# A two-layer graph-attention kernel: all scores of a quad and all attentions of the preceding quad in one bundle over eight PSUM banks, rows finished two steps behind

## The reference, cut to what matters

```python
def layer(x, adj, Wq, bq, Wk, bk, Wv, bv):          # layer 1; layer 0 also has Wo, bo
    q = (x @ Wq + bq).reshape(b, n, H, HD)          # H = 8, HD = 64; k and v alike
    scores = jnp.einsum('bihd,bjhd->bhij', q, k) / jnp.sqrt(jnp.float32(HD))
    scores = scores + mask[None, None, :, :]        # -1e9 where adj == 0
    weights = jax.nn.softmax(scores, axis=-1)
    return jnp.einsum('bhij,bjhd->bihd', weights, v).reshape(x.shape)
x = _layernorm(x + layer0(x) @ Wo + bo)
x = _layernorm(x + layer1(x))
```

## Time and profile before

| | |
|---|---|
| median of three runs | 3045.7 us |
| the profiled execution | 3046.8 us |
| its span, first to last instruction | 3045.0 us |
| TensorE busy | 3000.5 us (99%) |
| VectorE busy | 1915.4 us (63%) |
| ScalarE busy | 1560.9 us (51%) |
| GpSimd busy | 1366.4 us (45%) |
| mean granted TensorE clock | 0.994 of full speed |

### The profile page before, as it was taken

One profiled execution on the slowest core, in us unless ns is written; L12 is line 12 of the kernel. 1 busy time (PEld: TensorE's weight loads), 2 busy tenths in 40 slices (PEclk: granted clock), 3 DMA queues, 4 the chain that ended last, 5 costly groups with the idle time before them and its releaser, 6 DMA issues.

```text
span 3045.0 us, 58516 instructions
## 1 busy us (share of the span) xinstructions
PE 3000.5 (99%) x18956; PEld 2464.5 (81%) x18956; DVE 1915.4 (63%) x7060; ACT 1560.9 (51%) x5135; POOL 1366.4 (45%) x1285
## 2 busy tenths in 40 slices
PE   8999999999999999999999999999999999999996
PEld 6888888888888888888888888888888888888885
DVE  4656656565656566565656666666667666667665
ACT  4353535454444535353545556555556555565553
POOL 3454545545454545445454534343433333434332
PEclk9999999999999999999999999999999999999997
DMA  4443444444444445344445555555555555555554
GB/s 147 117 133 106 135 114 125 116 120 120 124 125 124 126 112 136 107 130 120 119 119 148 145 160 147 147 155 161 147 162 149 148 154 158 150 162 151 148 156 125
DMA packets 410914, 414.58 MB, mean 136 GB/s; under 512 B 46064, under 2 KB 308464, under 8 KB 410608
## 3 DMA queue, kind: packets, MB, share of 16 engines
q1 hardware_dynamic: 409312, 410.17, 48.8%
q10 hardware_dynamic: 1296, 0.67, 0.1%
HBM read 142.22 MB, written 100.66 MB: 80 GB/s over the span
## 4 chain that ended last, share of the span: by engine, by line
PE 98%; issue 1%; DVE 0%; DMA 0%; ACT 0%; SPq 0%; POOL 0%; POOLq 0%; DVEq 0%
PE ring L307 47%; PE ring L315 35%; PE ps_score L342 8%; PE ring L353 8%; DMA prob<-w_k 0%; DVE prob L628 0%; ACT k_all L487 0%; PE ps_score L315 0%; DMA prob_t<-turned 0%; DVE turned L646 0%; POOL rstd L829 0%; SPq L207 0%; DVE stats L681 0%; DVE x_res L676 0%; DVE w_lo_k L591 0%
## 5 line engine op out<-in xcount | busy, mean ns | idle before, releaser
L506 ACT ACTIVATE prob<-prob,neg_max 128x128 f32<-128x128 f32 x2048 | 791.7, 389 | 182.7 <-DVE neg_max L628 182.7
L822 POOL TENSOR_TENSOR prob<-prob,inv_sum 128x512 f32<-128x512 f32 x512 | 527.7, 1052 | 546.3 <-DVE inv_sum L636 546.3
L494 ACT ACTIVATE q_all<-ring,bq_col 128x512 f32<-128x512 f32 x256 | 176.6, 690 | 900.2 <-PE ring L307 900.2
L829 POOL TENSOR_TENSOR rstd<-var_eps,minus_half 128x1 f32<-128x1 f32 x256 | 169.5, 662 | 859.2 <-DVE var_eps L685 858.5
L628 DVE CUSTOM_DVE_ANT_0 prob<-ps_score,mask 128x128 f32<-128x128 f32 x2048 | 442.5, 285 | 153.6 <-PE ps_score L342 153.4
L646 DVE STREAM_TRANSPOSE turned<-prob 128x512 f32<-128x512 f32 x512 | 343.0, 696 | 305.7 <-DMA prob_t<-turned 214.5
L812 POOL TENSOR_TENSOR xt_lo<-x_raw,xt_hi 128x512 fp32r<-128x512 f32 x254 | 339.3, 1343 | 243.9 <-DVE xt_hi L603 243.9
L307 PE MATMUL ring<-xt_hi,w_hi_k 128*128 128x512 f32 x1024 | 399.0, 390 | 14.9 <-DVE w_lo_k L591 14.9
L307 PE MATMUL ring<-xt_hi,w_hi_q 128*128 128x512 f32 x1024 | 413.0, 403 | 0.0
L315 PE MATMUL ring<-w_hi_v,xt_hi 128*128 128x512 f32 x1024 | 412.7, 403 | 0.0
L307 PE MATMUL ring<-xt_lo,w_hi_q 128*128 128x512 f32 x1024 | 399.9, 391 | 0.0
(11 more groups left out here) (66 smaller groups left out, 4707.3 us busy)
## 6 DMA issues: line engine op xcount, KB each, us to landing
prob_t<-turned SPq DMA_DIRECT2D x1024, 128.0 KB, 2.7
x_res<-x_tok SPq DMA_DIRECT2D x256, 256.0 KB, 3.0
x_raw<-x_feat SPq DMA_DIRECT2D x254, 256.0 KB, 3.1
x_feat<-x_turned SPq DMA_DIRECT2D x512, 64.0 KB, 2.1
x_tok<-x_bias SPq DMA_DIRECT2D x128, 256.0 KB, 2.3
prob_t<-x_bias SPq DMA_DIRECT2D x512, 64.0 KB, 2.2
out<-x SPq DMA_DIRECT2D x128, 256.0 KB, 2.6
prob<-w_k SPq DMA_DIRECT2D x2, 512.0 KB, 7.7
```

What stands on the lines that cost most here:

```text
L494: act.activation(q_all[:, m, :], ring[bank][:], ACT.Identity, bias=bq_col[layer][:, m:m + 1]).then_inc(q_set, 1)
L506: last = act.activation(prob[b][:, i, n, :], prob[b][:, i, n, :], ACT.Exp, bias=neg_max[b][:, i, n:n + 1], scale=-1.0, accum_out=row_sum[b ...
L822: pool.tensor_tensor(prob[b][:, i], prob[b][:, i], inv_sum[b][:, i, :].unsqueeze(2).to_broadcast([P, NC, NODES]), ALU.mult).then_inc(norm_ ...
```

## The change

The eight PSUM banks become one ring. The scores of a quad take all eight (`score_bank(b, e)` is bank 2b + e). In a step TensorE runs keys (banks 7, 4, 5, 6), queries (banks 0 to 3), the values of graph 0 (bank 7), the scores of all four graphs, right behind them the attentions of all four graphs of quad a = s - 1 (banks 0 to 3, each as soon as the scores that lay there are masked), the values of graphs 1 to 3 (banks 4 to 6), and in layer 0 the four out projections. The four small bundles of a step become one of 128 instructions.

The rows of a quad are finished a step later, f = s - 2, so there is a step more (66). That takes more buffers: the high and low attention parts are there for each graph (`at_hi`, `at_lo`), the values of graph 0 twice (`v_first`), and the carried attention of layer 1 goes into `at_lo[b]` instead of `prob_t[b]`. `w_new` is given up for room; the second-layer weights are copied to internal DRAM tensors in step 0, and in step 31 loaded into the low-part buffers and split there, all six halves at the end of the step.

The order on the other engines is changed with it. DVE in step s: turn_blocks of graphs 2 and 3 of quad a between the finishes of quad f, then all four `x_high` of quad s + 1, then all masks of quad s, then the attentions of quad a. SP in step s: two raw loads, turn_probs(a, 2), the stores of graphs 0 and 1 of quad f, turn_probs(a, 3), the stores of graphs 2 and 3, the other two raw loads, turn_probs(s, 0), carries 0 and 1, turn_probs(s, 1), carries 2 and 3. POOL and ACT follow the same order. Waits that changed are shown below.

```diff
 # TensorE
+                    for m in range(NC):
+                        if m == 0:
+                            need(pe, masked_set, 2 * QB * s)
+                        else:
+                            need(pe, v_set, QB * a + m + 1)
+                        keys(s, m)
...
+                        if layer_of(s - 2) == 0:
+                            pe.wait_ge(sum_set, QB * (s - 2) + m + 1)
+                        elif layer_of(s - 2) == 1:
+                            pe.wait_ge(scaled_set, QB * (s - 2 - G) + m + 1)
+                        queries(s, m)
...
+                    values(s, 0)
+                    pe.wait_ge(q_set, NC * s + NC)
+                    scores(s, 0)
+                    scores(s, 1)
+                    scores(s, 2)
+                    pe.wait_ge(v_set, QB * s + 1)
+                    scores(s, 3)
+                if la is not None:
+                    for b in range(QB):
+                        if lp is not None:
+                            pe.wait_ge(masked_set, 2 * QB * s + b + 1)
+                        else:
+                            pe.wait_ge(scaled_set, QB * (a - 1 - G) + b + 1)
+                        attend(a, b)
+                if lp is not None:
+                    for b in range(1, QB):
+                        pe.wait_ge(masked_set, 2 * QB * s + 4 + b)
+                        values(s, b)
...
+                if la == 0:
+                    for b in range(QB):
+                        project_out(a, b)
 # SP
+            def step(s):
+                a, f = s - 1, s - 2
+                la, lf, nxt = layer_of(a), layer_of(f), layer_of(s + 1)
+                if nxt is not None:
+                    load_raw(s + 1, 0, nxt)
+                    load_raw(s + 1, 1, nxt)
                 if la is not None:
                     turn_probs(a, 2)
+                if lf is not None:
+                    finished(f, 0)
+                    finished(f, 1)
+                if la is not None:
                     turn_probs(a, 3)
+                if lf is not None:
+                    finished(f, 2)
+                    finished(f, 3)
...
                 if nxt is not None:
                     load_raw(s + 1, 2, nxt)
                     load_raw(s + 1, 3, nxt)
...
+                if s == 0:
+                    for n in SECOND:
+                        sp.dma_start(w_next[n], wts[n]).then_inc(w_next_out, 16)
+                if s <= LAST:
+                    turn_probs(s, 0)
                 if la == 1:
                     carry_attention(a, 0)
                     carry_attention(a, 1)
+                if s <= LAST:
+                    turn_probs(s, 1)
+                if la == 1:
                     carry_attention(a, 2)
                     carry_attention(a, 3)
 # DVE
+            def step(s):
+                a, f = s - 1, s - 2
+                lp, la, lf = layer_of(s), layer_of(a), layer_of(f)
                 if la is not None:
                     turn_blocks(a, 2)
+                if lf is not None:
+                    finish_start(f, 0)
+                if la is not None:
                     invert_sums(a, 3)
+                if lf is not None:
+                    finish_start(f, 1)
+                if la is not None:
                     turn_blocks(a, 3)
+                if lf is not None:
+                    finish_end(f, 0)
+                    finish_end(f, 1)
+                    finish_start(f, 2)
+                    finish_start(f, 3)
+                    finish_end(f, 2)
+                    finish_end(f, 3)
...
+                if s + 1 <= LAST:
+                    for b in range(QB):
+                        x_high(s + 1, b, x_raw[b % 2])
+                if lp is not None:
+                    mask_scores(s, 0, lp)
+                    mask_scores(s, 1, lp)
+                    mask_scores(s, 2, lp)
+                    invert_sums(s, 0)
+                    mask_scores(s, 3, lp)
+                    turn_blocks(s, 0)
+                for b in range(QB):
+                    if la == 0:
+                        attention_low(a, b)
+                    elif la == 1:
+                        turn_attention(a, b)
+                    if lp is not None and b == 1:
+                        invert_sums(s, 1)
+                if lp is not None:
+                    turn_blocks(s, 1)
+                    invert_sums(s, 2)
 # ACT
+                    values_out(s, 0)
+                    exps(s, 0)
+                    exps(s, 1)
+                for b in range(QB):
+                    if la == 0:
+                        attention_high(a, b)
+                    elif la == 1:
+                        attention_out(a, b)
+                if lp is not None:
+                    exps(s, 2)
+                    values_out(s, 1)
+                    values_out(s, 2)
+                    exps(s, 3)
+                    values_out(s, 3)
```

More of the change, by code:

```diff
@@ L154, in raw_view, with layer_of, v_of, score_bank @@
             return t[:].rearrange("p (r c t) -> p r c t", r=BLK, c=NC)
-        def all_steps(eng, step):
-            for s in range(2 * G + 1):
-                step(s, s % 2, None if s > LAST else s // G, None if s == 0 else (s - 1) // G)
+        def layer_of(quad):
+            return quad // G if 0 <= quad < 2 * G else None
+        def v_of(quad, b):
+            return v_first[quad % 2] if b == 0 else v_other[b - 1]
+        def score_bank(b, e):
+            return ring[2 * b + e][:].rearrange("p (c n) -> p c n", c=NC)
         def by_head(t):
@@ L229, in store_y, with finished @@
                 sp.dma_start(out[a - G, b], x1[b % 2][:]).then_inc(y_out[b % 2], 16)
[L231 to L243, removed]
+            def finished(f, b):
+                if layer_of(f) == 0:
+                    store_x1(f, b)
+                else:
+                    store_y(f, b)
+                if f + 1 <= LAST:
+                    load_res(f + 1, b)
+            def step(s):
+                a, f = s - 1, s - 2
+                la, lf, nxt = layer_of(a), layer_of(f), layer_of(s + 1)
                 if nxt is not None:
@@ L293, in _ @@
             for b in range(QB):
-                load_res(0, b, 0)
-            all_steps(sp, step)
+                load_res(0, b)
+            for s in range(2 * G + 2):
+                step(s)
             for i in range(2):
@@ L583, in _ @@
             act.wait_ge(small_in, 16 * 9)
-            all_steps(act, step)
+            for s in range(2 * G + 1):
+                step(s)
         @block.vector
@@ L704, in turn_x1, with finish_start @@
                 dve.transpose(x1_turned[b % 2][:], x1[b % 2][:]).then_inc(x1_turned_set, 1)
-            def step(s, par, lp, la):
-                a = s - 1
-                first = s == 0
-                more = lp is not None and not (s == LAST)
-                def next_x(b):
-                    if more:
-                        x_high(s + 1, b, 1 - par, x_raw[b % 2])
-                def finish_start(b, bank):
-                    if la == 0:
-                        residual0(a, b, bank)
-                    else:
-                        residual1(a, b)
-                    statistics(a, b)
-                def finish_end(b):
-                    normalise(a, b, la)
-                    if la == 0:
-                        turn_x1(a, b)
+            def finish_start(f, b):
+                if layer_of(f) == 0:
+                    residual0(f, b)
+                else:
+                    residual1(f, b)
+                statistics(f, b)
@@ L799, in _ @@
             for b in range(QB):
-                x_high(0, b, 0, first_raw[b])
+                x_high(0, b, first_raw[b])
             for i in range(4):
@@ new lines, in step @@
+                if lf is not None:
+                    inverse_deviation(f, 1)
+                    if lf == 0:
+                        add_value_bias(f, 0)
+                        add_value_bias(f, 1)
+                    inverse_deviation(f, 2)
+                    inverse_deviation(f, 3)
+                    if lf == 0:
+                        add_value_bias(f, 2)
+                        add_value_bias(f, 3)
+                if s + 1 <= LAST:
+                    for b in range(QB):
+                        x_low(s + 1, b, x_raw[b % 2])
@@ L883, in _ @@
             for b in range(QB):
-                x_low(0, b, 0, first_raw[b])
-            all_steps(pool, step)
+                x_low(0, b, first_raw[b])
+            for s in range(2 * G + 2):
+                step(s)
 def kernel(**inputs):
```

485 lines of the change are left out of this document (144 added, 341 removed).

## The result

The changed kernel takes 3164.7 us (median of four runs, 3163.5 to 3167.7) against 3045.9 for the kernel before beside it: ratio 1.0391, interval 1.0378 to 1.0404. It is slower, as forecast, but by 119 us and not by 27, and outside the range. The profiled execution spans 3163.2 us; the prediction's sum was 3072.3.

A forecast was written before the change was run, and what follows sets the result against it. In layer 1 the DVE and SP loop, 43.3 us a step, was to bound the kernel: 1720.3 to step 33's first mask, 29 loops +1255.7, then 38.8 and 57.5, span 3072.3. Forecast 3073, range 3010 to 3122.

The forecast's parts named there:

- TensorE's part: TensorE's work per step with one merged bundle: 0.98 us saved, layer-0 step 51.2 us, layer-1 step 40.33.
- The bundle: 64 score and 64 attend instructions on TensorE in one bundle: 7.70 us taken, between 7.53 and 7.89, against 8.68 before.
- the middle switch: Change from 64-row score tiles to 64-column attend tiles inside the merged bundle: between nothing and 0.36 us.
- The loop as the bound: In layer 1 the DVE and SP loop takes 43.3 us a step against TensorE's 40.33; TensorE waits 3.0 us.
- The first rival: TensorE stays the bound everywhere, if the last raw load lands before M+39.9: 2991 us profiled, chance 0.15.
- M: Start of the first mask of quad s on DVE; times in a step count in us from it.
- The landing times: Time for DMAs on the layer-1 loop to land: 2.6 us for the store, 3.0 for the last raw load.
- The cast: DVE's last cast before the masks, x_high(3), beside POOL's x_low(2): 1.02 us instead of 0.43.
- The start: Run up to the first mask of step 33; second-layer weight copies and v1 weights taken at 0, allowed 0 to 8 each.
- M33: First mask of step 33, forecast at 1720.3 us; M with another number is the first mask of that step.
- The tail: From the first mask of step 63 to the end: 57.5 us, some 9.7 longer as rows finish two steps behind.
- the long loop: Layer-1 step of 45 us, groups of issues at 2.87, landings above their medians: 3124; chance 0.16 together with no saving.

The follow-up runs named there:

- x_both_res: Changed kernel with casts of graphs 0 and 1 and the last two raw loads early, layer-1 residual loads behind the last store: 2990.6 us, 0.9814.
- res_less: Changed kernel with layer-1 residual loads bringing 128 of 512 columns, same number and order of DMAs: 3137.7 us, 1.0296.
- res_last: Changed kernel with the four layer-1 residual loads issued behind the last raw load instead of one behind each store: 3096.2 us, 1.0149.
- low_late: Changed kernel with POOL's x_low of graph 2 only after the cast of graph 3: 3141.0 us, 1.0305.
- w_o_early: Changed kernel with ACT's two casts of the out-projection weights ahead of queries_out in step 0: 3162.5 us, 1.0381.
- best_w_o: x_both_res with ACT's two casts of the out-projection weights ahead of queries_out in step 0: 2989.2 us, 0.981.
- x_dve: Changed kernel with DVE and POOL casting and splitting graphs 0 and 1 before finishing rows 2 and 3, SP's order kept: 3158.7 us, 1.0368.
- y_four: Changed kernel with four output rows instead of two in layer 1, so no finish waits for a store of its own quad: 3169.1 us, 1.0397.

## Why the prediction was right or wrong

**TensorE's part: right.** 51.17 us in layer 0, and 40.29 in layer 1 wherever nothing waits (x_both_res; forecast 40.33). The bundle: 3.77 + 3.64 in the chain, and behind it 36 full matmuls take 8.39 where 36 x 0.2267 (21.76 for 96) are 8.16, so 0.23 for the exit, 7.64 in all (7.70 taken). With 0.056 and 0.055 each, 64 scores are 3.58, so the way in costs 0.19; 64 attentions are 3.52, so the middle switch costs 0.12, inside the bounds of nothing to 0.36. The Trainium skill (TensorEngine Tiling (Array Packing), Key Properties) says that a change of tiling mode drains the engine; by equal shares of 0.2 three changes gave 0.6, the runs show 0.54.

**The loop as the bound: right in place and order.** The wait of 3.0 us in front of `attend` is there (3.5), the 4 points up to the store's issue hold to 0.3 us, and from there to the last raw load SP stands still only for x_low, twice, 0.5 and 0.7 us. The first rival (TensorE bounds everywhere) needed the last load by M+39.9; it comes at 44.6. That the changed bundle can bound is shown by x_both_res, a span of 2989.7 against the rival's 2989.3, once the rest is reordered.

**The landing times: wrong, and this is the step that failed.** The prediction took 2.6 us for the store and 3.0 for the raw load, the medians of the earlier trace rows, and the durations of a trace in which the raw loads stand ahead of the stores. It counted SP's issues one by one but not that they now follow each other for 14 us: four raw loads, eight DMAs of turn_probs, four stores and four residual loads, of which three kinds are 256 KB each. The store took 4.07 (+1.47) and the raw load 3.78 (+0.78) on average. The share of 0.96 and 309 GB/s at M+34 to M+39 point to why, and res_less shows it for the store: with three quarters of the residual bytes gone it lands in 3.10. res_last takes 0.9 off the store and 0.45 off the load.

Part of the store's error was in the old trace already. The 2.6 of the earlier trace rows is a median over all four stores of a quad, and the one on the loop is that of graph 1: in the kernel before it took 3.5 us on average in quads 36 to 59 and never less than 3.07, the other three 2.3 to 2.8. The Trainium skill (DMA: Bandwidth & Descriptors, Latency and other measured facts) gives the access time of HBM as 0.2 us on average and 2 us at high load; the two landings that grew by 1.47 and 0.78 us lie within what that allows. No run here shows which part of a DMA grew, nor why the last raw load hardly gained in res_less.

**The cast: too small by 0.4.** 1.02 was one row of a cast that met only the end of an x_low. Two loads that land 0.65 us apart make it meet the whole of one, 1.39, about as long as the x_low itself (1.28); low_late puts 0.8 to 1.0 us on it. The Trainium skill (SBUF — State Buffer, SBUF: two separate sides) states an exclusive lock on a port pair that VectorE (in its two-port modes) and GpSimd share, held for the whole instruction by the one that starts first, while the other waits. The timelines agree in kind: 0.43 us alone, 1.44 beside an x_low that began 0.1 us earlier. By that rule the cast would take the rest of the x_low and then its own 0.43, 1.6 us (an estimate from those rows); it took less than that, and more than the 1.0 in the sum. Which mode the cast runs in no row shows. Store, load, cast and 0.1 of the rest make the 2.7 a step, 78 us in 29 steps.

**The start: wrong by about 7.** "I take 0 for both": the prediction priced the weight copies on SP's queue and the v1 weights, and did not see that ACT's casts of w_o had moved behind `queries_out`, with DVE's `first_low(6)`, the x casts of quad 1 and then the first masks queued behind them. With that edit alone (w_o_early) M31 comes 7.1 us earlier and M33 5.5 of its 10.6; the first period fell by 8. The other edge, the second-layer weights at s=31, was taken at 0 as well: M31 to M33 took 105.0 us instead of 102.3, 2.7 more, and the chain runs there through the six subtractions of `second_low` (2.36 us for two of them) and then the finish of rows and SP's line behind them, up to the next raw load. In x_both_res, where the casts and loads don't stand behind that line, the two steps take 102.3. The edge was inside the 0 to 8 us allowed; it was not tried alone. With both cured, M33 is 1721.6 in best_w_o (forecast 1720.3).

**The tail: right.** 58.2 from M63 against 57.5. The extra 10 us of rows finished two steps behind are in it. The 1.7 us between M62 and M63 are TensorE's clock: the 64 attentions of step 62 take 5.11 us from the first start to the last, at full clock 3.44. In res_last, where that bundle takes 3.44, M62 to M63 is 38.79 (forecast 38.8).

**The chances.** 45 us a step was in the text as the long loop, with 3124 and "landings above their medians", at 0.16 together with another case. Its upper end used 2.87 us a group and no price for a queue filled by neighbours; both bounds came from a trace in which that crowd does not occur, so the range ended 43 us short. The branches add up to 0.06 for the same and 0.72 for slower, where the text has 0.07 and 0.71.

The version to use is x_both_res, 2990.6 us, 1.9% faster than the kernel before; with the w_o casts early 2989.2, which can't be told from it.

## What to carry to other kernels

When, as here, a change puts loads, stores and probabilities next to each other on one queue, a landing time taken from the old trace no longer holds: add up the bytes that are issued in the stretch before the load that closes the loop, and compare them with the GB/s that the DMA engines reach. A load that is needed late and stands in front of one that is needed now is the first thing to move. Take the landing time of the very DMA that is on the loop, not the median of its kind. And draw up the orders of the other engines from the new deadline before judging a merged bundle: here the same merge was worth +3.9% or -1.9% by where six DMAs, two casts and two low parts of each step stood. And for step 0 follow the one-time instructions of every engine, not SP's alone.

## What the runs showed that was not expected

A later or earlier issue did not move the landing: load_raw(3) issued at M+39.8, 40.2 and 40.85 landed at M+44.5, 44.9 and 44.6 (x_dve, y_four, the changed kernel). The waits in front of `attend` also cost TensorE pace: in the row of M to M+8, behind a wait of 3.4 us, its granted clock is 0.57, so near the lower of its two levels (1.2 of 2.4 GHz), and the 64 attentions took 6.4 us instead of 3.64. On average over layer 1 a bundle lost 2.0 us this way and waited 3.5: 40.3 + 2.0 + 3.5 is the 45.8 between first scores. In a loop of 46 us TensorE had the slack for it, so it did not lengthen the loop. In res_last 13 of 30 bundles run at the low clock (5.0 to 6.1 us) and the rest at full (3.71), and the periods between first scores go between 41 and 47 us. The length of the wait alone does not tell which: there the clock stayed full behind 3.0 and 3.3 us from the last score's start to the first attend's, and fell behind 2.2.
